# The attention loop of layers 1 to 3: scores copied by ScalarE, maximum on VectorE, subtraction on GpSimd

## The chip, the cores and the metric

The kernel runs on one core of a Trainium2 chip. The metric is the time of one execution on the device, in microseconds (us). Smaller is better. The engines are TensorE (matmul and transpose, results in PSUM), VectorE, ScalarE, GpSimd and SyncE, which only starts transfers here. Each engine works through its own list of instructions in order, and waits for the others on semaphores.

## The reference

Four layers, each a cross-attention from 2048 tokens (2 sequences of 1024, width 256) to 64 context rows per sequence, and then a feed-forward part (a plain and a routed one, experts, an FP4-quantised one, experts with a shared part). What the change touches is the attention of layers 1, 2 and 3. Here it is for layer 2; layer 1 is the same, layer 3 also has a mask.

```python
q = query @ Wq + bq
k = key @ Wk + bk
v = value @ Wv + bv
# 16 heads of 16 numbers
scores = jnp.einsum('bhqd,bhkd->bhqk', q, k) / jnp.sqrt(HEAD_DIM)
attn = jax.nn.softmax(scores, axis=-1)
out = jnp.einsum('bhqk,bhkd->bhqd', attn, v)
return out.transpose(0, 2, 1, 3).reshape(B, S, D_MODEL) @ Wo + bo
# and around it: x = x + tanh(g_xattn[l]) * attention(layernorm(x), context)
```

Layer 0 differs in one thing that matters: a bias from memory is added to its scores.

## The kernel before

The program is a row of phases with a barrier after most of them; `attention(l)` is built four times, once a layer. Everything stays in on-chip memory: X holds the tokens (16 tiles of 128 tokens), FA and RA are two large scratch areas. The weights, keys and queries are split into a high and a low part, and a product of two such operands is three matmuls (`split_matmuls`, L254).

After the queries of all tiles are there, each engine runs the same loop over slots. In slot s an engine does, in an order written by hand in its `work` function, its share for several tiles at once:

- TensorE (L802): transposes of the probabilities of tile s (L810); scores of a later tile, 12 small matmuls (L833), in layer 3 with four mask matmuls ahead of them (L826); transposes of the normalised output of tile s-1 (L842); product with V of tile s (L849); output projection of tile s-1 (L254), which waits for `ot_split`.
- ScalarE (L628): copy of the transposed probabilities of tile s out of PSUM (L631, into `pt`); high part of the transposed output of tile s-1 (L634, `ot`); exponential of tile s+1 (L639), which waits for `sub_done`.
- VectorE (L722): reciprocal of the row sums and normalisation of tile s-1 (L727, L728); output bias and residual of tile s-2 (L740, L742); maximum over each head's 64 scores and subtraction of it, for the tile that is LEAD ahead; low part of the transposed output of tile s-1 (L762), which waits for `ot_hi` and signals `ot_split`.

The tile of scores is 128 x 1024 numbers: 16 heads by 64 context rows. It lies in two of the eight PSUM banks, and there are two such pairs. In layers 1 to 3 LEAD is 1: VectorE reads the scores of tile s+1 in PSUM twice, for the maximum (L758) and for the subtraction (L759), whose result goes to one of two `probs` buffers. GpSimd has no part in these loops. In layer 0 LEAD is 2: VectorE adds the bias to the scores of tile s+2 while it moves them to one of three `probs` buffers (L750), takes the maximum there (L756), and GpSimd subtracts it (L572). TensorE computes scores LEAD+1 tiles ahead. Slots run from -LEAD-1 to 17.

The loop of layer 0 is written out slot by slot. In layers 1 to 3 `slots` writes out the first and the last slots and puts slots 2 to 11 of ScalarE and VectorE in a hardware loop of two slots a turn, whose counts of semaphores are computed in registers. TensorE's list is written out in all layers.

Of the kernel before, what the change touches and what calls it, by code (L numbers as in the profile page):

```python
# [76 lines left out]
def build(nc, A, out, stop=99):  # L77
    with ExitStack() as ctx:
# [368 lines left out]
        def attention(l):  # L447
# [10 lines left out]
            BUFS = 3 if first else 2  # L458
# [26 lines left out]
            bias_free, max_ready = shared(n_ + "biasfree"), shared(n_ + "max")  # L485
# [6 lines left out]
            LEAD = 2 if first else 1  # L492
            FIRST_SLOT, LAST_SLOT = -LEAD - 1, NT + 1
            LOOP = (1, NT // 2 - 2)
# [24 lines left out]
            def slots(eng, work, steps=None, per_slot=0):  # L519
                if first:  # L520
                    for t in range(FIRST_SLOT, LAST_SLOT + 1):
                        work(Slot(t - t % 2, t % 2), steps)
                    return steps.base + steps.n if steps else 0

                for t in range(FIRST_SLOT, 2 * LOOP[0]):
                    work(Slot(t - t % 2, t % 2), steps)
                before = steps.base + steps.n if steps else 0
                with eng.Fori(2 * LOOP[0], 2 * LOOP[1], 2) as t:
                    if steps:
                        steps = Steps(eng, dve_steps, per_slot * t + (before - 2 * per_slot * LOOP[0]))  # L530
                    for p in range(2):
                        work(Slot(t, p), steps)
                    assert not steps or steps.n == 2 * per_slot, (steps.n, per_slot)
                if steps:
                    steps = Steps(eng, dve_steps, before + 2 * per_slot * (LOOP[1] - LOOP[0]))
                for t in range(2 * LOOP[1], LAST_SLOT + 1):
                    work(Slot(t - t % 2, t % 2), steps)
                return steps.base + steps.n if steps else 0
# [25 lines left out]
            def gpsimd(pool):  # L564
                if first:
                    kv.gpsimd(pool)
                norm.gpsimd(pool)
                if first:
                    for t in range(NT):
                        pr = probs[t % BUFS].rearrange("p (h s) -> p h s", s=S2)  # L570
                        pool.wait_ge(max_ready, t + 1)
                        pool.tensor_tensor(pr, pr, mx[t % 2].unsqueeze(2).to_broadcast([P, H, S2]), ALU.subtract).then_inc(sub_done, 1)  # L572

            def scalar(act):
# [53 lines left out]
                def work(slot, steps):  # L628
                    if slot.has(0):
                        slot.wait(act, pt_ready, 0, 1)  # L630
                        act.activation(pt, PS[:, 4:6, :].rearrange("p b (c t) -> p (b c) t", t=P), ACT.Copy).then_inc(pt_sb, 1)  # L631
                    if slot.has(-1):
                        slot.wait(act, ot_ready, -1, 1)
                        act.activation(ot[:, 0], PS[:, 7, 0:D].rearrange("p (k t) -> p k t", k=KC), ACT.Copy).then_inc(ot_hi, 1)  # L634
                    if slot.has(1):
                        t, p = slot.tile(1)
                        slot.wait(act, sub_done, 1, 1)
                        pr = probs[t % BUFS] if first else probs[p]
                        act.activation(pr, pr, ACT.Exp).then_inc(p_ready, 1)  # L639
# [3 lines left out]
            def vector(dve):  # L643
# [78 lines left out]
                def work(slot, steps):  # L722
# [20 lines left out]
                    if slot.has(LEAD):  # L743
                        t, p = slot.tile(LEAD)
                        sc = PS[:, 2 * p:2 * p + 2, :].rearrange("p k (h s) -> p (k h) s", s=S2)
                        pr = (probs[t % BUFS] if first else probs[p]).rearrange("p (h s) -> p h s", s=S2)
                        slot.wait(dve, s_ready, LEAD, 1)
                        if first:
                            dve.wait_ge(bias_here[p], 16 * (t // 2 + 1))
# [4 lines left out]
                            if t >= 2:  # L754
                                dve.wait_ge(sub_done, t - 1)
                            dve.tensor_reduce(mx[p], pr, AX, ALU.max).then_inc(max_ready, 1)  # L756
                        else:
                            steps(dve.tensor_reduce(mx[p], sc, AX, ALU.max))  # L758
                            dve.tensor_tensor(pr, sc, mx[p].unsqueeze(2).to_broadcast([P, H, S2]), ALU.subtract).then_inc(sub_done, 1)  # L759
# [5 lines left out]
                per_slot = 3  # L765
                taken[0] = slots(dve, work, steps, per_slot)

            def tensor(pe):
# [33 lines left out]
                def work(slot, steps):  # L802
# [10 lines left out]
                    if slot.has(LEAD + 1):  # L813
# [3 lines left out]
                        if t >= 2:  # L817
                            if first:
                                pe.wait_ge(bias_free, 2 + t - 1)
                            else:  # L820
                                slot.wait(pe, sub_done, 2, -1)
# [1767 lines left out]
```

## Time and profile before

| | us |
|---|---|
| median of 3 runs | 1744.93 |
| lowest, highest run | 1736.59, 1745.95 |
| profiled execution, its own time | 1738.02 |
| profiled execution, its span | 1736.3 |

| engine, over the span | busy us | share |
|---|---|---|
| TensorE, matmuls | 1429.2 | 82% |
| TensorE, weight loads (overlap the matmuls) | 1329.2 | 77% |
| VectorE | 1301.9 | 75% |
| ScalarE | 734.3 | 42% |
| GpSimd | 364.7 | 21% |

The profile names the TensorE clock that was granted, as a share of 2.4 GHz; it has two levels, 1.00 and 0.50 (1.2 GHz), and was 0.887 on the average of the span. The shares above are averages over very different phases. The four attention loops take about 78 us of the span in layer 0, 87 and 86 in layers 1 and 2 and 97 in layer 3, and only layers 1 to 3 have code that the change touches. In the rows further down PE is TensorE's matmul, PEld its weight load, DVE VectorE, ACT ScalarE and POOL GpSimd. A bracket at the end of a row tells how long the engine had been idle before it and what ended that.

### The profile page before, as it was taken

What the parts mean: (1) busy time and instruction counts of PE and PEld (TensorE: products, weight loads), DVE (VectorE), ACT (ScalarE), POOL (GpSimd) and SP (SyncE); (2) the same over time, 40 slices, a digit from 0 to 9 for tenths busy, and PEclk for the clock granted to TensorE, in tenths of its full rate; (3) what the DMA queues carried; (4) which work ended last, traced back from release to release, by engine and by line L of the source; (5) the groups of instructions that cost most, each with busy time, mean ns of one, the idle gap of its engine ahead of it and who ended that gap; (6) DMA issues with size and microseconds to landing.
All of it is one profiled execution on the core that took longest, in us unless ns stands there. A gap on an engine that the chain in (4) does not pass through costs nothing.

```text
span 1736.3 us, 27180 instructions
## 1 busy us (share of the span) xinstructions
PE 1429.2 (82%) x10234; PEld 1329.2 (77%) x10234; DVE 1301.9 (75%) x2433; ACT 734.3 (42%) x1203; POOL 364.7 (21%) x290
## 2 busy tenths in 40 slices
PE   5894997897975799995894138977989999999995
PEld 4793886686965799995793137976878889999995
DVE  5777778778787487773888877987777848888882
ACT  4442341202433277773451312324433226766762
POOL 2231001001000167773000000001000013544532
PEclk8996998898995699998897558988996999999998
DMA  3231100000002477874001000000002027777783
GB/s 131 97 98 65 55 1 1 1 1 10 1 37 91 158 212 228 237 214 90 8 1 56 0 1 1 1 1 10 1 10 89 1 85 242 210 225 222 209 227 73
DMA packets 46675, 147.70 MB, mean 85 GB/s; under 512 B 11427, under 2 KB 24406, under 8 KB 36950
## 3 DMA queue, kind: packets, MB, share of 16 engines
q1 hardware_dynamic: 28918, 122.30, 20.1%
q0 software_dynamic: 17664, 24.13, 8.1%
q8 instruction: 62, 1.02, 0.2%
q14 instruction: 31, 0.25, 0.0%
HBM read 125.96 MB, written 22.54 MB: 86 GB/s over the span
## 4 chain that ended last, share of the span: by engine, by line
PE 71%; DVE 20%; ACT 3%; DMA 2%; issue 2%; POOL 1%; POOLq 1%; SPq 0%; DVEq 0%; ACTq 0%
PE PS L254 48%; PE PS L849 7%; PE PS L810 3%; PE PS L833 3%; PE PS L937 2%; DVE stats L182 2%; PE PS L230 2%; PE PS L1081 1%; PE PS L842 1%; DVE Y L2251 1%; DVE Y L2250 1%; PE PS L1442 1%; DVE FA L2252 1%; DVE Y L2243 1%; DVE FA L2237 1%
## 5 line engine op out<-in xcount | busy, mean ns | idle before, releaser
L254 PE MATMUL PS<-RA 128*128 128x256 f32 (+3 forms) x6456 | 967.5, 310 | 63.5 <-DVE RA L343 15.9
L254 PEld LDWEIGHTS PS<-RA 128*128 128x128 f32 x6456 | 887.8, 196 | 112.7 <-issue 27.2
L1353 POOL DMA_INDIRECT sum_rows<-Y,KT x92 | 164.1, 1784 | 185.7 <-ACT Y L1390 166.8
L1342 POOL DMA_INDIRECT Y<-normed_rows,KT x92 | 116.0, 1261 | 226.6 <-DVE KT L1156 157.8
L218 POOL TENSOR_TENSOR rstd<-vareps,neghalf 128x4 f32<-128x4 f32 x36 | 40.7, 1130 | 561.8 <-DVE vareps L187 453.9
L849 PE MATMUL PS<-VBF,FA 128*128 128x136 f32 x1024 | 135.6, 286 | 5.4 <-ACT FA L631 5.4
L849 PEld LDWEIGHTS PS<-VBF,FA 128*128 128x128 f32 x1024 | 124.1, 191 | 11.3 <-ACT FA L631 7.5
L1421 DVE TENSOR_TENSOR RA<-FA,RA 128x2048 fp32r<-128x2048 f32 x46 | 105.2, 2288 | 20.3 <-ACT RA L1382 20.3
L230 PE MATMUL PS<-ident,FA 128*128 128x128 f32 x160 | 33.5, 379 | 98.1 <-DVE FA L2252 40.7
L1369 ACT ACTIVATE FA<-PS,unit_bias 128x256 f32<-128x256 f32 x184 | 77.4, 476 | 86.7 <-PE PS L254 82.9
L631 ACT ACTIVATE FA<-PS 128x1024 f32<-128x1024 f32 x64 | 65.6, 1026 | 111.7 <-PE PS L810 111.7
L230 PEld LDWEIGHTS PS<-ident,FA 128*128 128x128 f32 x160 | 27.6, 198 | 103.7 <-issue 75.4
L1382 ACT ACTIVATE RA<-FA 128x2048 fp32r<-128x2048 f32 x46 | 88.1, 1915 | 18.8 <-DMA FA<-in_eup 18.8
L1487 DVE TENSOR_TENSOR RA<-FA,RA 128x1024 fp32r<-128x1024 f32 (+1 forms) x46 | 80.9, 1759 | 19.8 <-ACT RA L1414 19.8
L639 ACT ACTIVATE FA<-FA 128x1024 f32<-128x1024 f32 x64 | 67.5, 1055 | 40.5 <-DVE FA L759 35.1
L237 ACT ACTIVATE RA<-PS 128x512 fp32r<-128x512 f32 x64 | 36.7, 596 | 110.3 <-PE PS L230 110.2
L1805 DVE SCALAR_TENSOR_TENSOR X<-PS,coef,X 128x256 f32<-128x256 f32 x128 | 61.5, 483 | 25.8 <-PE PS L254 23.5
L810 PE MATMUL PS<-ident,FA 128*128 128x128 f32 x512 | 68.4, 278 | 12.0 <-ACT FA L639 12.0
L1414 ACT ACTIVATE RA<-FA 128x1024 fp32r<-128x1024 f32 (+1 forms) x46 | 68.5, 1489 | 0.0
L810 PEld LDWEIGHTS PS<-ident,FA 128*128 128x128 f32 x512 | 58.0, 143 | 12.8 <-ACT FA L639 12.8
L1462 DVE TENSOR_TENSOR RA<-FA,RA 128x512 fp32r<-128x512 f32 x92 | 63.7, 693 | 3.2
L833 PE MATMUL PS<-RA 64*128 64x256 f32 x768 | 63.6, 301 | 1.1 <-DVEq L753 1.1
(249 smaller groups left out, 1932.7 us busy)
## 6 DMA issues: line engine op xcount, KB each, us to landing
FA<-in_eup SPq DMA_DIRECT2D x46, 1024.0 KB, 7.4
FA<-in_edown SPq DMA_DIRECT2D x23, 1024.0 KB, 6.3
FA<-in_edown SPq DMA_DIRECT2D x23, 512.0 KB, 3.7
FA<-in_fside SPq DMA_DIRECT2D x16, 512.0 KB, 3.3
sum_rows<-X SPq DMA_DIRECT2D x2, 2048.0 KB, 7.4
normed_rows<-Y SPq DMA_DIRECT2D x2, 2048.0 KB, 7.2
X<-in_x SPq DMA_DIRECT2D x4, 512.0 KB, 9.2
FA<-in_up SPq DMA_DIRECT2D x4, 512.0 KB, 3.8
```

The costliest lines, as they stand in the source:

```text
L230: ins = pe.transpose(self.bank(g, k)[:, j * P:(j + 1) * P], self.normed(g, j)[:, 0, k * P:(k + 1) * P], ident[:, :])
L254: ins = pe.matmul(dst, stat(a, k), mov(b, k), start=(first and n == 0), stop=(last and n == len(todo) - 1))
L810: ins = pe.transpose(PS[:, 4 + c // 4, (c % 4) * P:(c % 4 + 1) * P], probs[t % BUFS][:, c * P:(c + 1) * P], ident[:, :])
L833: ins = pe.matmul(PS[:, 2 * p + r, k * COLS:(k + 1) * COLS], qs[rows, a, k, t * P:(t + 1) * P], kb[rows, b, m, k, r * COLS:(r + 1) * COLS] ...
L849: ins = pe.matmul(PS[:, 6, k * VC:(k + 1) * VC], pt[:, 4 * (c // 2) + 2 * k + c % 2, :], VB[:, t // HT, 4 * k + c, :], start=(c == 0), sto ...
L1342: pool.indirect_dma_start(out=rows_in[p][:, t, :], out_offset=None, in_=normed_rows, in_offset=bass.IndirectOffsetOnAxis(ap=source_of[:, R ...
L1353: pool.indirect_dma_start(out=sum_rows, in_=rows_out[p][:, t, :], in_offset=None, compute_op=ALU.add, out_offset=bass.IndirectOffsetOnAxis ...
L1369: ins = act.activation(h32[s % RING][:, c * BR:(c + 1) * BR], bank[:, c * BR:(c + 1) * BR], ACT.Relu, bias=unit_bias[:, p, 2 * s + c:2 * s ...
L1382: act.activation(up[q][:, 0], raw_up[q], ACT.Copy).then_inc(up_hi, 1)
L1414: act.activation(down[p][:, 0], raw_down[p], ACT.Copy).then_inc(down_hi, 1)
L1421: dve.tensor_tensor(up[q][:, 1], raw_up[q], up[q][:, 0].bitcast(F32), ALU.subtract).then_inc(up_ready, 1)
L1487: dve.tensor_tensor(down[p][:, 1], raw_down[p], down[p][:, 0].bitcast(F32), ALU.subtract).then_inc(down_ready, 1)
```

## The change

In layers 1 to 3:

- ScalarE copies the scores of tile s+2 from PSUM to a `probs` buffer, between the `ot` part of tile s-1 and the exponential of tile s+1. It signals the new semaphore `s_moved`.
- VectorE takes the maximum of tile s+2 from that buffer, after it has waited for `s_moved`. It no longer subtracts.
- GpSimd subtracts the maximum, in place.
- LEAD is 2, there are three `probs` buffers, and TensorE's scores of tile s+3 wait for `s_moved` of tile s+1 where they waited for `sub_done`.
- The hardware loop goes; all slots are written out.

Layer 0 keeps its code.

```diff
-            BUFS = 3 if first else 2
+            BUFS = 3
-            LEAD = 2 if first else 1
+            LEAD = 2
...
-            def slots(eng, work, steps=None, per_slot=0):
-                if first:
...
+            def slots(eng, work, steps=None):
+                for t in range(FIRST_SLOT, LAST_SLOT + 1):
                     work(Slot(t - t % 2, t % 2), steps)
                 return steps.base + steps.n if steps else 0
...
-                if first:
-                    for t in range(NT):
...
+                for t in range(NT):
+                    pr = probs[t % BUFS].rearrange("p (h s) -> p h s", s=S2)
+                    pool.wait_ge(max_ready, T + t + 1)
+                    pool.tensor_tensor(pr, pr, mx[t % 2].unsqueeze(2).to_broadcast([P, H, S2]), ALU.subtract).then_inc(sub_done, 1)
...
                         act.activation(ot[:, 0], PS[:, 7, 0:D].rearrange("p (k t) -> p k t", k=KC), ACT.Copy).then_inc(ot_hi, 1)
+                    if not first and slot.has(LEAD):
+                        t, p = slot.tile(LEAD)
+                        slot.wait(act, s_ready, LEAD, 1)
+                        act.activation(probs[t % BUFS].rearrange("p (r n) -> p r n", r=ROWTILES), PS[:, 2 * p:2 * p + 2, :], ACT.Copy
+                                       ).then_inc(s_moved, 1)
...
                     if slot.has(LEAD):
...
-                            steps(dve.tensor_reduce(mx[p], sc, AX, ALU.max))
-                            dve.tensor_tensor(pr, sc, mx[p].unsqueeze(2).to_broadcast([P, H, S2]), ALU.subtract).then_inc(sub_done, 1)
+                            dve.wait_ge(s_moved, NT * (l - 1) + t + 1)
+                        if t >= 2:
+                            dve.wait_ge(sub_done, T + t - 1)
+                        dve.tensor_reduce(mx[p], pr, AX, ALU.max).then_inc(max_ready, 1)
...
                             else:
-                                slot.wait(pe, sub_done, 2, -1)
+                                pe.wait_ge(s_moved, NT * (l - 1) + t - 1)
```

ScalarE's list in the last written-out slots of layer 1, before. A slot is three rows (`at_pt`, `at_ot` and `at_sub` are the semaphores `pt_ready`, `ot_ready` and `sub_done`):

```order
155 L631 ACTIVATE FA<-PS 128x1024 [waits at_pt]
156 L634 ACTIVATE RA<-PS 128x256 [waits at_ot]
157 L639 ACTIVATE FA<-FA 128x1024 [waits at_sub]
158 L631 ACTIVATE FA<-PS 128x1024 [waits at_pt]
159 L634 ACTIVATE RA<-PS 128x256 [waits at_ot]
160 L639 ACTIVATE FA<-FA 128x1024 [waits at_sub]
```

The same engine and layer in the change. A slot is four rows, lines L613, L616, L620 and L626 of the changed file:

```order
178 L613 ACTIVATE FA<-PS 128x1024 [waits at_pt]
179 L616 ACTIVATE RA<-PS 128x256 [waits at_ot]
180 L620 ACTIVATE FA<-PS 128x1024 [waits at_s]
181 L626 ACTIVATE FA<-FA 128x1024 [waits at_sub]
182 L613 ACTIVATE FA<-PS 128x1024 [waits at_pt]
183 L616 ACTIVATE RA<-PS 128x256 [waits at_ot]
184 L620 ACTIVATE FA<-PS 128x1024 [waits at_s]
185 L626 ACTIVATE FA<-FA 128x1024 [waits at_sub]
```

The copy of the scores (L620, waiting for `s_ready`) stands between the `ot` part and the exponential.

VectorE's list in one slot of layer 1, before: L727 and L728 normalise, L740 and L742 are bias and residual, L758 and L759 maximum and subtraction, L762 the low part of `ot`.

```order
541 L727 RECIPROCAL small<-PS 128x16 [waits at_o]
542 L728 TENSOR_TENSOR FA<-PS,small 128x256 [waits dve_steps]
543 L740 TENSOR_TENSOR FA<-PS,FA 128x256 [waits at_y]
544 L742 SCALAR_TENSOR_TENSOR X<-FA,gates,X 128x256 [waits dve_steps]
545 L758 TENSOR_REDUCE small<-PS 128x16 [waits at_s]
546 L759 TENSOR_TENSOR FA<-PS,small 128x1024 [waits dve_steps]
547 L762 TENSOR_TENSOR RA<-PS,RA 128x256 [waits at_othi]
```

And one slot of it in the change, where the lines are L714, L715, L727, L729, L744 (maximum) and L747 (`ot`):

```order
509 L714 RECIPROCAL small<-PS 128x16 [waits at_o]
510 L715 TENSOR_TENSOR FA<-PS,small 128x256 [waits dve_steps]
511 L727 TENSOR_TENSOR FA<-PS,FA 128x256 [waits at_y]
512 L729 SCALAR_TENSOR_TENSOR X<-FA,gates,X 128x256 [waits dve_steps]
513 L744 TENSOR_REDUCE small<-FA 128x16 [waits at_sub,at_smoved]
514 L747 TENSOR_TENSOR RA<-PS,RA 128x256 [waits at_othi]
```

The subtraction is gone, and the maximum, which waited for the scores of TensorE, now waits for `s_moved` of ScalarE and for `sub_done` of an earlier tile. The low part of `ot` still stands behind it.

## Rows read from the trace of the kernel before

**Rows 1.** Stretches (layer 1, layer 0, end of layer 1): us, busy per engine, granted clock, DMA

```profile
446.00:494.60 48.60, 48.60 (x442) 44.79 (x441) 42.93 (x71) 24.68 (x30) 0.00 (x0) 1.00 0.01 1
73.50:117.00 43.50, 43.50 (x399) 40.02 (x398) 34.25 (x55) 21.27 (x28) 17.48 (x10) 1.00 0.34 111
505.40:508.80 3.40, 2.69 (x22) 2.25 (x21) 1.90 (x5) 1.50 (x3) 0.00 (x0) 1.00 0.00 0
```

**Rows 2.** Chain of waits, 446 to 456 us (layer 1): its shares by line

```profile
by line: PE PS L849 42.7%; PE PS L833 18.2%; PE PS L810 17.5%; PE PS L254 15.1%; PE PS L842 7.4%
```

**Rows 3.** In order of time, layer 1: start us, us, engine, line, operation [idle before]

```profile
447.55 0.86 PEld L810 LDWEIGHTS PS<-ident,FA 128*128 128x128 f32 x8
...
448.68 1.02 ACT L631 ACTIVATE FA<-PS 128x1024 f32<-128x1024 f32 x1 [1.18 <-PE PS L810]
...
449.75 1.92 PEld L849 LDWEIGHTS PS<-VBF,FA 128*128 128x128 f32 x16
...
449.95 0.38 ACT L634 ACTIVATE RA<-PS 128x256 fp32r<-128x256 f32 x1 [0.25 <-PE PS L842]
...
450.04 1.22 DVE L759 TENSOR_TENSOR FA<-PS,small 128x1024 f32<-128x1024 f32 x1
...
451.18 0.41 DVE L762 TENSOR_TENSOR RA<-PS,RA 128x256 fp32r<-128x256 f32 x1
...
451.65 0.78 PEld L254 LDWEIGHTS PS<-RA 128*128 128x128 f32 x6
...
452.41 0.86 PEld L810 LDWEIGHTS PS<-ident,FA 128*128 128x128 f32 x8
```

**Rows 4.** In order of time, layer 0, the same columns

```profile
74.66 0.90 PEld L810 LDWEIGHTS PS<-ident,FA 128*128 128x128 f32 x8
...
76.67 1.22 DVE L756 TENSOR_REDUCE small<-FA 128x16 f32<-128x1024 f32 x1 [0.16 <-DVE FA L750]
...
77.11 0.38 ACT L634 ACTIVATE RA<-PS 128x256 fp32r<-128x256 f32 x1 [0.25 <-PE PS L842]
...
77.39 1.05 ACT L639 ACTIVATE FA<-FA 128x1024 f32<-128x1024 f32 x1
...
77.97 1.90 POOL L572 TENSOR_TENSOR FA<-FA,small 128x1024 f32<-128x1024 f32 x1 [2.63 <-DVE small L756]
...
79.08 0.26 DVE L727 RECIPROCAL small<-PS 128x16 f32<-128x16 f32 x1 [0.85 <-PE PS L849]
...
79.49 0.90 PEld L810 LDWEIGHTS PS<-ident,FA 128*128 128x128 f32 x8
```

**Rows 5.** Line L727 in layer 2, ns min/median/max, first and last start

```profile
L727 DVE RECIPROCAL small<-PS x11: 256/258/260, 864.6 to 913.2; 128x16 f32<-128x16 f32 x11
```

**Rows 6.** In order of time, layer 3, the same columns

```profile
1238.51 0.90 PEld L810 LDWEIGHTS PS<-ident,FA 128*128 128x128 f32 x8
...
1241.91 0.38 ACT L634 ACTIVATE RA<-PS 128x256 fp32r<-128x256 f32 x1 [1.19 <-PE PS L842]
...
1244.17 0.90 PEld L810 LDWEIGHTS PS<-ident,FA 128*128 128x128 f32 x8
```

**Rows 7.** In order of time, slot 14 of layer 1

```profile
500.87 0.90 PEld L810 LDWEIGHTS PS<-ident,FA 128*128 128x128 f32 x8
...
502.97 0.38 ACT L634 ACTIVATE RA<-PS 128x256 fp32r<-128x256 f32 x1
```

**Rows 8.** In order of time, starts of the loops of layers 1 and 3

```profile
427.45 0.69 ACT L586 ACTIVATE RA<-PS,small 128x512 fp32r<-128x512 f32 x1 [0.67 <-PE PS L254]
...
428.84 1.22 DVE L758 TENSOR_REDUCE small<-PS 128x16 f32<-128x1024 f32 x1
...
432.45 0.85 PEld L810 LDWEIGHTS PS<-ident,FA 128*128 128x128 f32 x8 [3.63 <-ACT FA L639]
...
435.02 2.85 PEld L849 LDWEIGHTS PS<-VBF,FA 128*128 128x128 f32 x16 [0.22 <-issue]
...
1201.88 1.22 DVE L758 TENSOR_REDUCE small<-PS 128x16 f32<-128x1024 f32 x1 [0.70 <-PE PS L833]
```

More of the change, by code:

```diff
@@ L484, in attention @@
             bias_here = [shared(n_ + f"bias{i}") for i in range(2)]
-            bias_free, max_ready = shared(n_ + "biasfree"), shared(n_ + "max")
+            bias_free, max_ready, s_moved = shared(n_ + "biasfree"), shared(n_ + "max"), shared(n_ + "smoved")
             norm = Norm(TURNS[f"at{l}"], X, xn, *[lambda g, k, a=a: xt[:, a, k, g % 2, :] for a in range(2)])
@@ L488, in attention @@
             Q = KC * NG * l
-            LEAD = 2 if first else 1
+            LEAD = 2
             FIRST_SLOT, LAST_SLOT = -LEAD - 1, NT + 1
-            LOOP = (1, NT // 2 - 2)
             class Slot:
@@ L517, in wait @@
                         eng.wait_ge(s, count)
-            def slots(eng, work, steps=None, per_slot=0):
-                if first:
[L521 to L536, printed above, removed]
+            def slots(eng, work, steps=None):
+                for t in range(FIRST_SLOT, LAST_SLOT + 1):
                     work(Slot(t - t % 2, t % 2), steps)
@@ L567, in gpsimd @@
                 norm.gpsimd(pool)
-                if first:
-                    for t in range(NT):
-                        pr = probs[t % BUFS].rearrange("p (h s) -> p h s", s=S2)
-                        pool.wait_ge(max_ready, t + 1)
-                        pool.tensor_tensor(pr, pr, mx[t % 2].unsqueeze(2).to_broadcast([P, H, S2]), ALU.subtract).then_inc(sub_done, 1)
+                for t in range(NT):
+                    pr = probs[t % BUFS].rearrange("p (h s) -> p h s", s=S2)
+                    pool.wait_ge(max_ready, T + t + 1)
+                    pool.tensor_tensor(pr, pr, mx[t % 2].unsqueeze(2).to_broadcast([P, H, S2]), ALU.subtract).then_inc(sub_done, 1)
             def scalar(act):
@@ L637, in work @@
                         slot.wait(act, sub_done, 1, 1)
-                        pr = probs[t % BUFS] if first else probs[p]
+                        pr = probs[t % BUFS]
                         act.activation(pr, pr, ACT.Exp).then_inc(p_ready, 1)
@@ L744, in work @@
                         t, p = slot.tile(LEAD)
-                        sc = PS[:, 2 * p:2 * p + 2, :].rearrange("p k (h s) -> p (k h) s", s=S2)
-                        pr = (probs[t % BUFS] if first else probs[p]).rearrange("p (h s) -> p h s", s=S2)
-                        slot.wait(dve, s_ready, LEAD, 1)
+                        pr = probs[t % BUFS].rearrange("p (h s) -> p h s", s=S2)
                         if first:
+                            slot.wait(dve, s_ready, LEAD, 1)
                             dve.wait_ge(bias_here[p], 16 * (t // 2 + 1))
@@ L753, in work @@
                             dve.sem_inc(bias_free, 1)
-                            if t >= 2:
-                                dve.wait_ge(sub_done, t - 1)
-                            dve.tensor_reduce(mx[p], pr, AX, ALU.max).then_inc(max_ready, 1)
-                        else:
-                            steps(dve.tensor_reduce(mx[p], sc, AX, ALU.max))
-                            dve.tensor_tensor(pr, sc, mx[p].unsqueeze(2).to_broadcast([P, H, S2]), ALU.subtract).then_inc(sub_done, 1)
+                        else:
+                            dve.wait_ge(s_moved, NT * (l - 1) + t + 1)
+                        if t >= 2:
+                            dve.wait_ge(sub_done, T + t - 1)
+                        dve.tensor_reduce(mx[p], pr, AX, ALU.max).then_inc(max_ready, 1)
                     if slot.has(-1):
@@ L763, in work @@
                                           ALU.subtract).then_inc(ot_split, 1)
-                per_slot = 3
-                taken[0] = slots(dve, work, steps, per_slot)
+                taken[0] = slots(dve, work, steps)
             def tensor(pe):
```

## The prediction

> **What bounds the kernel now.** I read the engine shares over the attention stretches first, then the chain of waits there, then the order of instructions in one slot (one pass of `work`, one tile of 128 tokens further along). In layer 1 TensorE's weight loads fill 44.79 of 48.60 us, its matmuls all of it, VectorE is busy 42.93, ScalarE 24.68, GpSimd not at all [rows 1]. VectorE looks almost as full as TensorE, so the reader should see which of the two is waited for: the chain of waits over two slots consists of TensorE lines alone [rows 2]. A slot takes 452.41 - 447.55 = 4.86 us, the distance between two groups of transposes (L810) [rows 3]. Layer 0 already works the way the change wants (scores copied to memory, maximum there, GpSimd subtracts), and its slot is 79.49 - 74.66 = 4.83 us [rows 4]. So both schemes stand at TensorE's pace, and the new one can win 0.03 us a slot at the most by relieving VectorE. Layer 2 is like layer 1: ten slots in 913.2 - 864.6 = 48.6 us, 4.86 each [rows 5]. Layer 3 (masked, four more matmuls a slot) takes 1244.17 - 1238.51 = 5.66 us [rows 6].
>
> TensorE's queue is in order: the transposes of slot s+1 stand behind the output projection (L254) of slot s, which waits for `ot_split`, VectorE's L762. Today L762 starts at 451.18 and L254 at 451.65, just when the product with V (L849, 16 loads of 1.92 us from about 449.75) is through [rows 3]. This cover is exactly used up: whatever makes L762 later moves TensorE one for one.
>
> **The change, part by part.**
>
> Removed from VectorE in each slot of layers 1 to 3: the subtraction L759, 1.22 us [rows 3]. The maximum stays at 1.22 us, now from memory as layer 0's L756 [rows 4]. VectorE was not the bound, so by itself this is worth nothing.
>
> Added to ScalarE: one copy of 128x1024 from PSUM. L631 is the same shape and direction, 1.02 us [rows 3]. ScalarE's load rises from 2.47 us a slot (24.68 over ten [rows 1]) to 3.5, inside 4.86. Added to GpSimd: the subtraction, 1.90 us as L572 [rows 4], also inside the slot.
>
> The place of the copy is what costs. In a slot s, ScalarE now runs: pt copy of tile s, `ot` high part of tile s-1 (L634), copy of scores s+2, exponential of s+1. VectorE runs: normalisation, residual, maximum of tile s+2, `ot` low part of tile s-1. Maximum and copy are of the same tile in the same slot, although the scores are two tiles ahead. So the maximum waits (on `s_moved`) until ScalarE has been through its pt copy, its `ot` part and its scores copy, and queued behind the waiting maximum stands the `ot` low part, for which TensorE's output projection waits, with the next transposes behind that. The buffers and the lead don't loosen this, since all of it lies within a slot. In layer 0 the copy's counterpart (the bias add) is VectorE's own and waits for no ScalarE work of the slot, which is why layer 0 doesn't show the loop.
>
> The new chain from one L810 to the next, for slots 1 to 12 of layers 1 and 2:
> - L810 to the start of L634: 77.11 - 74.66 = 2.45 us [rows 4] (2.40 in [rows 3]).
> - L634 to the next ScalarE operation, whose input is ready: 77.39 - 77.11 = 0.28 [rows 4].
> - the copy: 1.02.
> - copy to maximum: 0.16, the gap ahead of L756, which has a second wait as the new maximum has [rows 4]; the least hand-over in these rows is 0.05 (L631 ending 449.70, L849 starting 449.75 [rows 3]). I take the row of the like instruction.
> - maximum to the start of the `ot` low part: 451.18 - 450.04 = 1.14, as behind L759, which is as long [rows 3].
> - its start to L254: 451.65 - 451.18 = 0.47 [rows 3].
> - L254 to the next L810: 452.41 - 451.65 = 0.76 [rows 3].
> Sum 6.28 us, against 4.86: +1.42 a slot. The exponential of s+1 (starting at 2.45 + 0.28 + 1.02, 1.05 long [rows 4], so done by 4.8) and GpSimd's subtraction (5.2 to 7.1 us after the L810, needed two ScalarE operations into the next slot at 6.28 + 3.7) are off the path.
>
> Slot 13 still copies (tile 15) but has no scores to compute; L634 then follows the pt copy at 502.97 - 500.87 = 2.10 us as in slot 14 of layer 1 [rows 7], so it takes 2.10 + 3.83 = 5.93. Slot 0 has no `ot` part, slots 14 to 16 no copy: these keep their length. Per layer 1 or 2: 12 x 1.42 + (5.93 - 4.86) = 18.1 us.
> Layer 3: L634 starts 1241.91 - 1238.51 = 3.40 after L810 [rows 6], so a slot is 3.40 + 3.83 = 7.23 against 5.66; 12 x 1.57 + (5.93 - 5.66) = 19.1 us.
>
> The start of each loop: before, the first maximum starts at 428.84 and the first transposes at 432.45 [rows 8]. After, TensorE's first scores are read by the copy, then come maximum, GpSimd and exponential. Against the old way (maximum, subtraction, exponential) this adds the copy 1.02, the gap 0.16, and 1.90 + 0.08 for GpSimd (77.97 after the maximum's end at 77.89 [rows 4]) in place of 1.22 + 0.03: 1.91 us. In layers 1 and 2 ScalarE is free earlier than VectorE (428.14 against 428.84 [rows 8]), and the copy can start once the scores are there, between the two; I take 0.4 us of it, the bounds being 0 and 0.7. In layer 3 the maximum already waits for the scores (1201.88 [rows 8]), and nothing is gained. So +1.5 twice and +1.9 once: 4.9 us. The third tile of scores computed ahead of time fits into this wait.
>
> Writing the loop out takes away register work, worth at the most the 0.03 us a slot named above, and only if TensorE's pace ruled: zero here. More instructions are fetched; layer 0 is written out already and shows no cost of it.
>
> Sum: 18.1 + 18.1 + 19.1 + 4.9 = 60.2 us. With 0.05 in place of 0.16 at the gap and 2.40 in place of 2.45 it is 60.2 - 39 x 0.16 = 54; with what either can be too small by (another 0.05 at two of the hand-overs) 64. Against the profiled execution (1738.02 us, span 1736.3) this gives 1798; that execution lies 6.9 us under the median of the runs, 1744.93. I forecast a median, so 1744.93 + 60.2 = 1805.
>
> **Rivals.**
> 1. Not slower: TensorE's pace goes on ruling. The mechanism would be that the copy, the maximum and the `ot` low part end before the product with V does, that is the chain from L810 to L254 stays under 4.1 us. For it speaks that VectorE is at 88% and loses 1.22 us a slot. The Trainium skill, Perfetto Trace Analysis, section Optimizing Scalar/DVE Operations, holds that work may well be moved to ScalarE or even GpSimd where VectorE is saturated, which is this case's intent; the trace agrees on the load and not on the wait. Time: 39 x (4.48 - 4.86) = -15 if TensorE closed the gaps of its loads (44.79 over ten slots), +5 for the starts: 1735, faster; with layer 0's pace, -1 + 5: 1749, the same. Against it: 2.45 + 0.28 + 1.02 + 1.22 alone are 4.97.
> 2. GpSimd holds VectorE up while it subtracts. If VectorE's `ot` low part waited for the whole of the 1.90 us, each slot would be 8.2 us: 39 x 1.9 = +74 more, 1879. Against it: in layer 0 L727 starts at 79.08 in the middle of GpSimd's 77.97 to 79.87 and takes its usual 0.26 [rows 4]. The Trainium skill, same section, warns that the two share a read port, so that moving work between them might not help; by that rule this rival's time would come, by layer 0's row nothing.
> 3. TensorE's clock falls. The new slot leaves TensorE idle some 1.4 us before L254. In layer 1's first slot at the lower level (1.2 GHz) the loads of L849 took 2.85 us against 1.92 [rows 3, 8]: 1.48 times. TensorE's part of the new chain is about 3.2 us; if every slot ran so, +1.5 x 39 = 60 more, 1865; if one in four, +15, 1820. Against it: at the end of layer 1 TensorE was busy 2.69 of 3.40 us, 79%, and the granted clock stayed at 1.00 [rows 1]; the new slot gives about 4.8 of 6.3, 76%.
>
> **How the numbers follow.** Forecast 84% (1805, 54 to 64 us of loss on a base anywhere in the runs of before, 1736.6 to 1746: 1791 to 1810). Rival 1: 7%, of it 3 faster and 4 the same. Rival 2: 3%. Rival 3: 6%, most of it the case of one slot in four. The range takes in the forecast's spread and rival 3's smaller case: 1787 to 1822. A measurement of this kernel can tell about 0.5% (9 us) from no change. Faster 0.03, same 0.04, slower 0.93.
>
> **What the profile after would show.** VectorE's maximum in layers 1 to 3 should be waiting for the ScalarE copy, about 2 us in each slot; TensorE's L254 should be idle for `ot_split`, about 1.4 us in each of 13 slots a layer; L810 groups should be 6.3 us apart in layers 1 and 2 and 7.2 in layer 3; layer 0 should be as it was; the copy should take 1.03, the subtraction 1.90. The granted clock should stay at 1.00 in the loops. If L810 groups are 4.8 apart, the chain argument is wrong; if they are over 8, rival 2 holds; if matmuls are stretched, rival 3.

## The result, and the profile after

| | us |
|---|---|
| changed kernel, median of 4 runs | 1798.88 (1796.73 to 1800.08) |
| kernel before, median of 4 runs | 1741.66 (1736.59 to 1745.95) |
| ratio, with its 95% interval | 1.0336 (1.0310 to 1.0362) |
| profiled execution of the changed kernel, span | 1795.0 |

The change costs 57 us by the medians and 58.7 us by the two spans (1795.0 against 1736.3). The quotient of the two medians is 1.0329, inside the interval of the ratio. The same stretches as in [rows 1], of the changed kernel: layer 1 (463.5 to 500 us) and layer 3 (1260 to 1330 us). The columns are the stretch, its length, busy us of TensorE, its weight loads, VectorE, ScalarE and GpSimd, then the granted clock.

```profile
463.50:500.00 36.50, 30.44 (x266) 26.93 (x265) 18.30 (x36) 19.60 (x24) 11.33 (x7) 1.00 0.00 1
1260.00:1330.00 70.00, 58.82 (x479) 50.94 (x478) 30.15 (x60) 32.67 (x40) 18.74 (x10) 1.00 0.00 1
```

In layer 1 TensorE's matmuls now fill 30.44 of 36.50 us where they filled all of the time [rows 1]. No other engine took its place: VectorE is at 50%, ScalarE at 54%, GpSimd at 31%. When no engine is busy all of the time, what bounds the loop is a chain that passes through several of them. The chain of waits over three slots of layer 1, its shares by line:

```profile
by line: PE PS L254 20.7%; DVE small L744 19.3%; ACT FA L620 14.6%; PE PS L817 14.3%; PE PS L794 13.8%; ACT RA L616 6.1%; PE PS L826 6.0%; DVE RA L747 5.4%; issue 1.4%
```

Before, all of it was TensorE [rows 2]. Now VectorE's maximum (L744), ScalarE's copy of the scores (L620) and its `ot` part (L616) and VectorE's `ot` part (L747) make up 45%; the rest is TensorE's. One slot in order of time, the counterpart of [rows 3]: start, length, engine, line, operation, and in brackets how long the engine had been idle and for what.

```profile
469.62 0.90 PEld L794 LDWEIGHTS PS<-ident,FA 128*128 128x128 f32 x8
...
470.80 1.02 ACT L613 ACTIVATE FA<-PS 128x1024 f32<-128x1024 f32 x1 [2.59 <-PE PS L794]
...
472.06 0.39 ACT L616 ACTIVATE RA<-PS 128x256 fp32r<-128x256 f32 x1 [0.24 <-PE PS L826]
472.35 1.02 ACT L620 ACTIVATE FA<-PS 128x1024 f32<-128x1024 f32 x1
...
473.40 1.22 DVE L744 TENSOR_REDUCE small<-FA 128x16 f32<-128x1024 f32 x1 [2.53 <-ACT FA L620]
474.53 0.41 DVE L747 TENSOR_TENSOR RA<-PS,RA 128x256 fp32r<-128x256 f32 x1
474.70 1.91 POOL L554 TENSOR_TENSOR FA<-FA,small 128x1024 f32<-128x1024 f32 x1 [4.20 <-DVE small L744]
...
475.00 0.77 PEld L254 LDWEIGHTS PS<-RA 128*128 128x128 f32 x6 [1.21 <-DVE RA L747]
...
475.72 0.90 PEld L794 LDWEIGHTS PS<-ident,FA 128*128 128x128 f32 x8
...
476.48 0.49 DVE L729 SCALAR_TENSOR_TENSOR X<-FA,gates,X 128x256 f32<-128x256 f32 x1
```

The reader should follow the times downwards. The copy L620 ends at 473.37, the maximum L744 starts 0.03 us later after 2.53 us of waiting, L747 stands behind it although its own input (L616) had been there since 472.45, and TensorE's projection L254 has waited 1.21 us for L747. The next transposes come 475.72 - 469.62 = 6.10 us after the last ones. In layer 3 the same, in place of 5.66 us [rows 6]:

```profile
1280.20 0.90 PEld L794 LDWEIGHTS PS<-ident,FA 128*128 128x128 f32 x8
...
1283.58 0.38 ACT L616 ACTIVATE RA<-PS 128x256 fp32r<-128x256 f32 x1 [1.18 <-PE PS L826]
...
1286.51 0.78 PEld L254 LDWEIGHTS PS<-RA 128*128 128x128 f32 x6 [1.32 <-DVE RA L747]
...
1287.23 0.90 PEld L794 LDWEIGHTS PS<-ident,FA 128*128 128x128 f32 x8
```

A slot there is 1287.23 - 1280.20 = 7.03 us. The start of layer 1's loop, the counterpart of [rows 8]:

```profile
428.43 1.94 ACT L620 ACTIVATE FA<-PS 128x1024 f32<-128x1024 f32 x2 [0.22 <-PE PS L817]
429.50 0.78 PEld L817 LDWEIGHTS PS<-RA 64*128 64x128 f32 x12 [0.61 <-ACT FA L620]
...
430.85 3.76 POOL L554 TENSOR_TENSOR FA<-FA,small 128x1024 f32<-128x1024 f32 x2 [15.44 <-DVE small L744]
432.79 1.06 ACT L626 ACTIVATE FA<-FA 128x1024 f32<-128x1024 f32 x1 [2.42 <-POOL FA L554]
433.89 1.57 PEld L794 LDWEIGHTS PS<-ident,FA 128*128 128x128 f32 x8 [3.62 <-ACT FA L626]
```

From the first use of the scores (428.43) the chain goes over copy, maximum, GpSimd and exponential to the first transposes at 433.89.

Where the 58.7 us are, phase by phase (from the start of one phase's first statistics, L182, to the next one's, in both traces): attention of layer 1 17.2, of layer 2 18.9, of layer 3 19.8, the FP4 part between layers 2 and 3 2.9. Of the rest, the parts ahead of layer 1's attention differ by -0.9 to +0.4 and add up to 0.0, the others are within 0.2. The FP4 part has no changed instruction; its granted clock was 0.73 on the average, against 0.76 before. Why, the runs don't show: in the profiled executions of the other experiments this part is 0.0 to 4.4 us longer than before, by 1.1 with the written-out loops alone. So its 2.9 us, read from one execution of each kernel, can't be counted as a cost of the change.

### The profile page after: what moved, and what is told of

Read it like the earlier page. It is cut to its first block, busy times and chain, and to the rows that moved or that the text cites. A ratio compares the mean times of both kernels' runs of the same rounds, so it can differ in the third digit from the quotient of the medians.

```text
span 1795.0 us, 26949 instructions
## 1 busy us (share of the span) xinstructions
PE 1445.8 (81%) x10234; PEld 1335.9 (74%) x10234; DVE 1242.9 (69%) x2385; ACT 773.6 (43%) x1251; POOL 455.5 (25%) x338
## 4 chain that ended last, share of the span: by engine, by line
PE 65%; DVE 22%; ACT 6%; DMA 2%; issue 2%; POOL 1%; POOLq 1%; SPq 0%; DVEq 0%; ACTq 0%
PE PS L254 47%; PE PS L794 3%; PE PS L817 3%; PE PS L833 3%; DVE small L744 3%; ACT FA L620 2%; DVE stats L182 2%; PE PS L921 2%; PE PS L230 2%; PE PS L1065 1%; PE PS L826 1%; DVE Y L2235 1%; DVE Y L2234 1%; PE PS L1426 1%; ACT RA L616 1%
## 5 line engine op out<-in xcount | busy, mean ns | idle before, releaser
L254 PE MATMUL PS<-RA 128*128 128x256 f32 (+3 forms) x6456 | 972.0, 310 | 101.8 <-DVE RA L747 43.3
L254 PEld LDWEIGHTS PS<-RA 128*128 128x128 f32 x6456 | 891.0, 196 | 159.3 <-DVE RA L747 52.2
L554 POOL TENSOR_TENSOR FA<-FA,small 128x1024 f32<-128x1024 f32 x64 | 121.8, 1905 | 298.7 <-DVE small L744 298.6
L744 DVE TENSOR_REDUCE small<-FA 128x16 f32<-128x1024 f32 x64 | 77.9, 1220 | 132.0 <-ACT FA L620 129.3
L613 ACT ACTIVATE FA<-PS 128x1024 f32<-128x1024 f32 x64 | 65.6, 1025 | 157.2 <-PE PS L794 157.2
L794 PE MATMUL PS<-ident,FA 128*128 128x128 f32 x512 | 69.1, 280 | 11.7 <-ACT FA L626 11.7
L626 ACT ACTIVATE FA<-FA 128x1024 f32<-128x1024 f32 x64 | 67.6, 1057 | 8.8 <-POOL FA L554 8.8
L794 PEld LDWEIGHTS PS<-ident,FA 128*128 128x128 f32 x512 | 59.5, 144 | 12.5 <-ACT FA L626 12.5
```

What stands on the lines that cost most here:

```text
L254: ins = pe.matmul(dst, stat(a, k), mov(b, k), start=(first and n == 0), stop=(last and n == len(todo) - 1))
L794: ins = pe.transpose(PS[:, 4 + c // 4, (c % 4) * P:(c % 4 + 1) * P], probs[t % BUFS][:, c * P:(c + 1) * P], ident[:, :])
```

## The experiments

Theory A is that of the prediction: in each slot the `ot` low part stands in VectorE's queue behind a maximum that waits for ScalarE's copy. Theory B is that GpSimd's subtraction costs, by its length or by holding VectorE up. Theory C is TensorE's clock. In the table a slot is the distance of two groups of transposes in the middle of the loop.

| run | median us | ratio to before (95%) | slot, layers 1 and 2 | slot, layer 3 |
|---|---|---|---|---|
| before | 1741.66 | | 4.86 | 5.66 |
| changed | 1798.88 | 1.0336 (1.0310 to 1.0362) | 6.10 | 7.03 |
| copy_first | 1743.51 | 1.0019 (1.0003 to 1.0035) | 4.82 | 5.66 |
| copy_between | 1766.12 | 1.0147 (1.0117 to 1.0176) | 5.47 | 5.66 |
| low_part_first | 1759.62 | 1.0101 (1.0072 to 1.0130) | 5.41 | 5.65 |
| low_first_psum | 1746.19 | 1.0039 (1.0024 to 1.0054) | 4.83 | 5.65 |
| vector_subtracts | 1863.89 | 1.0688 (1.0646 to 1.0730) | 7.37, some 8.5 to 8.9 | 8.3 to 9.9 |
| pool_twice | 1803.55 | 1.0342 (1.0303 to 1.0380) | 6.10 | 7.03 |
| copy_twice | 1849.75 | 1.0607 (1.0559 to 1.0654) | 7.02, in each layer one of 8.21 | 7.9 to 9.5 |
| count_between | 1800.22 | 1.0322 (1.0282 to 1.0363) | 6.21 | 7.13 |
| before_written_out | 1738.83 | 0.9992 (0.9978 to 1.0006) | 4.81 | 5.66 |

Each ratio of an experiment is to runs of the kernel before on the same chip, whose median was 1738.6 to 1744.8, not the 1741.66 of the first row.

### The copy ahead of everything else in the slot

```diff
+                    if not first and slot.has(LEAD):
+                        t, p = slot.tile(LEAD)
+                        slot.wait(act, s_ready, LEAD, 1)
+                        act.activation(probs[t % BUFS].rearrange("p (r n) -> p r n", r=ROWTILES), PS[:, 2 * p:2 * p + 2, :], ACT.Copy
+                                       ).then_inc(s_moved, 1)
                     if slot.has(0):
                         slot.wait(act, pt_ready, 0, 1)
...
-                    if not first and slot.has(LEAD):
...
```

> The changed kernel, with one move in layers 1 to 3: ScalarE copies the scores of the tile two ahead as the first thing in the slot, ahead of the copy of the transposed probabilities. The scores are ready then, and the copy runs while TensorE transposes. Theory A: the maximum starts 0.9 us into the slot and is over before the high part is there, so TensorE's pace comes back: 4.83 and 5.66 us a slot, about 1746 us (1743 to 1751). Theory B: about 1799. If ScalarE's extra work were itself too much, the slot would be over 4.9 us here and in the kernel with the low part first.

Measured: 1743.51 us, slots of 4.82 and 5.66 us. Five rows of a slot of layer 1; L614 is the copy of the scores, L744 the maximum, L621 and L747 the `ot` parts:

```profile
466.35 1.02 ACT L614 ACTIVATE FA<-PS 128x1024 f32<-128x1024 f32 x1
...
467.50 0.90 PEld L794 LDWEIGHTS PS<-ident,FA 128*128 128x128 f32 x8
...
468.67 1.21 DVE L744 TENSOR_REDUCE small<-FA 128x16 f32<-128x1024 f32 x1
...
469.95 0.38 ACT L621 ACTIVATE RA<-PS 128x256 fp32r<-128x256 f32 x1 [0.25 <-PE PS L826]
...
470.37 0.43 DVE L747 TENSOR_TENSOR RA<-PS,RA 128x256 fp32r<-128x256 f32 x1 [0.49 <-ACT RA L621]
```

The copy starts before the slot's transposes, the maximum starts at 468.67, and the low part L747 now waits for nothing but the high part (469.95 plus 0.38, then 470.37). All operations of the changed kernel are there, with ScalarE's extra copy and GpSimd's subtraction. The place of the copy alone made 55 us. The kernel is still no faster than the one before: the interval of its ratio, 1.0003 to 1.0035, lies just above 1.

### The copy between the two other ScalarE copies

```diff
-                    if slot.has(-1):
-                        slot.wait(act, ot_ready, -1, 1)
...
                     if not first and slot.has(LEAD):
                         t, p = slot.tile(LEAD)
...
+                    if slot.has(-1):
+                        slot.wait(act, ot_ready, -1, 1)
...
```

> The changed kernel, with one move in layers 1 to 3: ScalarE copies the scores between the copy of the transposed probabilities and the high part of the transposed output, not behind both. Theory A, in numbers from the trace of the changed kernel: the copy starts 2.10 us after the transposes, not 2.73, so the maximum ends at 4.37, the low part starts at 4.28 and the projection at 4.75: a slot of 5.47 us in layers 1 and 2 (6.10 in the changed kernel, 4.86 before); in layer 3 the projection is no longer waited for and TensorE's own 5.66 us come back. Total about 1741.7 + 26 x 0.61 + 5 = 1762 us (1757 to 1767). Theory B: no change, about 1799.

```profile
471.14 0.90 PEld L794 LDWEIGHTS PS<-ident,FA 128*128 128x128 f32 x8
...
473.24 1.02 ACT L617 ACTIVATE FA<-PS 128x1024 f32<-128x1024 f32 x1
...
474.29 1.22 DVE L744 TENSOR_REDUCE small<-FA 128x16 f32<-128x1024 f32 x1 [1.90 <-ACT FA L617]
...
475.43 0.41 DVE L747 TENSOR_TENSOR RA<-PS,RA 128x256 fp32r<-128x256 f32 x1
...
475.89 0.77 PEld L254 LDWEIGHTS PS<-RA 128*128 128x128 f32 x6 [0.58 <-DVE RA L747]
...
476.61 0.46 PEld L794 LDWEIGHTS PS<-ident,FA 128*128 128x128 f32 x4
```

The copy (L617) starts 2.10 us after L794, the maximum 3.15, the low part 4.29, the projection 4.75, and the slot is 476.61 - 471.14 = 5.47 us, as worked out ahead (to 0.01 us). Layer 3 is back at TensorE's 5.66, since its projection comes later than 4.75 anyway. The time, 1766.12 us, is 4 above the expected one; the span of its profiled execution is 1759.1, and the runs went from 1760.78 to 1769.56. That the same edit moves two loops by different amounts, each by what its own pace leaves over, is the strongest evidence for theory A.

### The low part ahead of the maximum

```diff
+                    if not first and slot.has(-1):
+                        slot.wait(dve, ot_hi, -1, 1)
+                        dve.tensor_tensor(ot[:, 1], PS[:, 7, 0:D].rearrange("p (k t) -> p k t", k=KC), ot[:, 0].bitcast(F32),
+                                          ALU.subtract).then_inc(ot_split, 1)
                     if slot.has(LEAD):
...
-                    if slot.has(-1):
+                    if first and slot.has(-1):
```

> The changed kernel, with one move in layers 1 to 3: VectorE does the low part of the transposed output (the operation for which TensorE's output projection waits) ahead of the maximum that waits for ScalarE's copy, not behind it. All operations stay. Theory A (the low part is stuck in VectorE's queue behind the waiting maximum): TensorE's pace comes back, 4.83 us a slot in layers 1 and 2, 5.66 in layer 3; only the longer starts of the loops stay, about 5 us, so about 1746 us (1743 to 1751) where the kernel before takes 1741.7 and the changed one 1798.9. Theory B (GpSimd's subtraction, or the port it shares with VectorE, is what costs): nothing of it is moved, so 1790 or more. Theory C (TensorE's clock): the idle time would be gone too, so it can't be told from A here.

Measured: 1759.62 us, which is 14 us more than the 1746 of theory A and outside its range. Most of the loss is gone, but slots are 5.41 us, not 4.83. The chain of waits from 470 to 486 us has no projection in it any more:

```profile
by line: DVE X L729 24.1%; DVE small L748 22.9%; ACT FA L620 17.3%; ACT RA L616 9.6%; DVE FA L715 8.0%; PE PS L830 7.9%; DVE FA L727 6.4%; issue 4.3%; DVE small L714 3.3%
```

A slot of it; L748 is the maximum, L732 the low part:

```profile
477.36 0.87 PEld L798 LDWEIGHTS PS<-ident,FA 128*128 128x128 f32 x8
...
477.69 1.90 POOL L554 TENSOR_TENSOR FA<-FA,small 128x1024 f32<-128x1024 f32 x1 [3.50 <-DVE small L748]
...
478.15 0.41 DVE L727 TENSOR_TENSOR FA<-PS,FA 128x256 f32<-128x256 f32 x1
...
478.61 1.27 DVE L729 SCALAR_TENSOR_TENSOR X<-FA,gates,X 128x256 f32<-128x256 f32 x1
480.00 0.20 PEld L830 LDWEIGHTS PS<-ident,FA 128*128 128x128 f32 x2 [0.82 <-issue]
...
480.89 0.42 DVE L732 TENSOR_TENSOR RA<-PS,RA 128x256 fp32r<-128x256 f32 x1 [1.01 <-ACT RA L616]
...
482.77 0.87 PEld L798 LDWEIGHTS PS<-ident,FA 128*128 128x128 f32 x8
```

The residual update L729 takes 1.27 us. It took 0.48 before and in the changed kernel (476.48 above). It ends at 479.88, while GpSimd's subtraction (L554) ran from 477.69 to 479.59. The same holds in all 39 slots in which the two meet. L727, which also ran inside that time, took its usual 0.41. The transposes of the output, L830, wait for L729. So a second chain came up: maximum, normalisation, residual update, L830, high part, copy, maximum. In the changed kernel GpSimd starts at 474.70 and is through by 476.61. L729 starts 0.13 us before that, at 476.48, and still takes its 0.48 to 0.49 us, in all 39 slots, so this didn't show there. From this I formed theory D: a VectorE operation with both its operands in memory is held up while GpSimd works in memory. L729 is one; L727 has an operand in PSUM.

### The same with one operand of the residual update in PSUM

The kernel is that of the run before, with these lines changed on top:

```diff
-                            steps(dve.tensor_tensor(tmp, y, bo_row, ALU.add))
+                            steps(dve.tensor_tensor(y, y, bo_row, ALU.add))
...
-                            dve.scalar_tensor_tensor(x, tmp.unsqueeze(1), gates[:, l:l + 1], x, ALU.mult, ALU.add).then_inc(fin_done, 1)
+                            dve.scalar_tensor_tensor(x, y.unsqueeze(1), gates[:, l:l + 1], x, ALU.mult, ALU.add).then_inc(fin_done, 1)
```

> The run with the low part first gave slots of 5.41 us, not 4.83, and its trace shows the residual update (L729, which reads tmp and X, both in memory) taking 1.27 us in place of 0.48; it ends 0.3 us after GpSimd's subtraction does. Here that kernel is changed in one thing: the output bias is added in place in PSUM, so the residual update reads one operand from PSUM and one from memory. Theory D (an operation of VectorE with two operands in memory is held while GpSimd's subtraction runs, one with a single operand in memory is not): the update takes about 0.5 us, the chain through it is 5.41 - 0.8 = 4.6 us, under TensorE's pace, so slots of 4.83 us in layers 1 and 2 and 5.66 in layer 3, about 1744 us (1741 to 1750). Theory E (the update is late for another cause, its place in the slot or a wait): it stays at 1.27 us and the slot at 5.41, about 1760 us.

```profile
476.84 0.90 PEld L798 LDWEIGHTS PS<-ident,FA 128*128 128x128 f32 x8
...
477.10 1.90 POOL L554 TENSOR_TENSOR FA<-FA,small 128x1024 f32<-128x1024 f32 x1 [2.92 <-DVE small L748]
...
478.01 0.48 DVE L729 SCALAR_TENSOR_TENSOR X<-PS,gates,X 128x256 f32<-128x256 f32 x1
...
478.81 0.20 PEld L830 LDWEIGHTS PS<-ident,FA 128*128 128x128 f32 x2
```

L729 lies wholly inside GpSimd's subtraction (477.10 to 479.00) and takes 0.48 us, again in all 39 slots. The slot is 4.83 us, the time 1746.19. Theory D holds: the update was held because both its operands lay in memory while GpSimd worked there. The Trainium skill, SBUF — State Buffer, section "SBUF: two separate sides", says that a VectorE instruction with two SBUF inputs and a GpSimd instruction that reads SBUF exclude each other for the whole instruction, and that whichever starts first goes on. These two runs agree, 1.27 against 0.48 us.

### VectorE subtracts

```diff
-                for t in range(NT):
+                for t in range(NT if first else 0):
                     pool.wait_ge(max_ready, T + t + 1)
...
+                            steps(dve.tensor_reduce(mx[p], pr, AX, ALU.max))
+                            dve.tensor_tensor(pr, pr, mx[p].unsqueeze(2).to_broadcast([P, H, S2]), ALU.subtract).then_inc(sub_done, 1)
```

> The changed kernel, but in layers 1 to 3 VectorE subtracts the maximum itself, from memory, right behind the maximum; GpSimd does nothing in these loops. ScalarE still copies. Theory A: the subtraction, 1.22 us and a hand-over of 0.03, stands ahead of the low part too, so each of 39 slots gets 1.25 us longer: 7.35 us in layers 1 and 2, 8.29 in layer 3, +49 us; the starts lose about 2 us; about 1846 us. Theory B (GpSimd is what costs): faster than the changed kernel's 1799.

Measured: 1863.89 us. Theory B is out: without any work on GpSimd the loop got slower, and by the expected 1.25 us in most slots (7.37). The other 18 us weren't expected; the slots that are longer than 7.37 and 8.3 us add up to about 20 us in the profiled execution. Two pairs of rows from layer 1, and the stretches of layers 1 and 3:

```profile
460.57 0.78 PEld L254 LDWEIGHTS PS<-RA 128*128 128x128 f32 x6 [2.47 <-DVE RA L751]
...
461.29 1.36 PEld L798 LDWEIGHTS PS<-ident,FA 128*128 128x128 f32 x8
...
469.45 0.77 PEld L254 LDWEIGHTS PS<-RA 128*128 128x128 f32 x6 [2.58 <-DVE RA L751]
...
470.17 0.90 PEld L798 LDWEIGHTS PS<-ident,FA 128*128 128x128 f32 x8
```

```profile
446.00:526.00 80.00, 57.41 (x464) 50.88 (x466) 44.11 (x73) 33.22 (x41) 0.00 (x0) 0.94 0.00 1
1295.00:1390.00 95.00, 71.19 (x490) 61.44 (x489) 43.14 (x71) 33.67 (x42) 0.00 (x0) 0.87 0.00 1
```

The first L798 takes 1.36 us where it otherwise takes 0.90, and this slot is 470.17 - 461.29 = 8.88 us. The granted clock was 0.94 and 0.87 on the average of these stretches, so TensorE ran at 1.2 GHz for a part of them. TensorE was idle 2.47 us before L254 here, against 1.21 in the changed kernel, where the clock stayed at 1.00 in the middle of the loops. Rival 3 of the prediction is real, but in these runs it shows only where TensorE idles for longer than this change makes it.

### The copy twice

```diff
                         slot.wait(act, s_ready, LEAD, 1)
...
+                        act.activation(fview(4096, ROWTILES, COLS * KC), PS[:, 2 * p:2 * p + 2, :], ACT.Copy).then_inc(twice, 1)
                         act.activation(probs[t % BUFS].rearrange("p (r n) -> p r n", r=ROWTILES), PS[:, 2 * p:2 * p + 2, :], ACT.Copy
```

> The changed kernel, but in layers 1 to 3 ScalarE copies the scores twice, first into a spare buffer that nobody reads. Theory A: everything ahead of VectorE's maximum in a slot is on the path one for one. Two ScalarE operations in a row start 0.92 us apart or, with a wait of one for the other, about 1.05 us: 39 slots and 3 starts with 0.92 to 1.05 us more, +39 to +44 us, 1838 to 1843 us, slots of 7.0 to 7.15 us in layers 1 and 2. Theory B: no change.

Measured: 1849.75 us, slots of 7.02 in layers 1 and 2, which is 0.92 more than 6.10. One for one. In layer 3 the slots were 7.9 to 9.5 where 7.03 + 0.92 = 7.95 was due. The stretches of layers 1 and 3 show why:

```profile
445.00:505.00 60.00, 44.55 (x390) 39.50 (x387) 24.99 (x50) 36.22 (x44) 16.57 (x9) 1.00 0.00 1
1285.00:1380.00 95.00, 73.49 (x512) 63.06 (x510) 31.24 (x61) 45.15 (x55) 19.11 (x11) 0.87 0.00 1
```

Clock 1.00 in this stretch of layer 1, 0.87 in layer 3. Behind the stretch, from 515.0 to 523.2 us, it fell to 0.79 in layer 1 too: that is its one slot of 8.21 us. All the slots above 7.02 and 7.95 us add up to about 13 us, which makes up the 7 to 12 us above the expected range.

### GpSimd's subtraction twice

```diff
                     pool.wait_ge(max_ready, T + t + 1)
+                    if not first:
...
+                        pool.tensor_tensor(fview(4096, H, S2), pr, mx[t % 2].unsqueeze(2).to_broadcast([P, H, S2]), ALU.subtract
+                                           ).then_inc(twice, 1)
                     pool.tensor_tensor(pr, pr, mx[t % 2].unsqueeze(2).to_broadcast([P, H, S2]), ALU.subtract).then_inc(sub_done, 1)
```

> The changed kernel, but in layers 1 to 3 GpSimd does the subtraction twice, first into a spare buffer that nobody reads. Theory A: GpSimd is off the path. Its result is there 8.9 us after the transposes of the slot and wanted 9.75 us after them: no change in the slots (6.10 and 7.04 us), and 1.9 us more at the start of each loop, where the first exponential waits for it: about 1804 us. Theory B (GpSimd or the port it shares with VectorE): 39 slots with up to 1.9 us more, up to +74 us.

Measured: 1803.55 us, slots unchanged at 6.10 and 7.03. The increase lies in the starts: the attention phases of the profiled execution are 2.5, 1.4 and 3.0 us longer than in the changed kernel. (By the intervals the two times can't be told apart.) GpSimd has its slack in the loops, as worked out. The rows below are the residual update (L735) and the two subtractions (L558, L560):

```profile
472.78 0.48 DVE L735 SCALAR_TENSOR_TENSOR X<-FA,gates,X 128x256 f32<-128x256 f32 x1
472.86 2.17 POOL L560 TENSOR_TENSOR FA<-FA,small 128x1024 f32<-128x1024 f32 x1
...
477.10 1.90 POOL L558 TENSOR_TENSOR FA<-FA,small 128x1024 f32<-128x1024 f32 x1 [2.07 <-DVE small L750]
```

The second subtraction takes 2.17 us, 0.27 more than the first. It was due when L735 had just started, and it was GpSimd that was held this time. In the loops this is so in each of the 36 slots in which the two meet; where they don't, it takes 1.90 us.

### A count between wait and maximum

```diff
                             dve.wait_ge(s_moved, NT * (l - 1) + t + 1)
+                            dve.sem_inc(shared(n_ + "spare"), 1)
```

> The changed kernel, but in layers 1 to 3 VectorE increases a spare semaphore between the wait for the copy and the maximum, as layer 0 increases bias_free between its add and its maximum. The prediction took 0.16 us for the hand-over from copy to maximum, from layer 0; the changed kernel shows 0.03 with two waits. If the increase between is what costs 0.13 us, the gap ahead of the maximum is 0.16 us here and 39 slots are 0.13 us longer: +5 us, about 1804 us. If not, the gap stays 0.03 and the slot 6.10.

```profile
471.47 1.02 ACT L620 ACTIVATE FA<-PS 128x1024 f32<-128x1024 f32 x1
...
472.63 1.22 DVE L745 TENSOR_REDUCE small<-FA 128x16 f32<-128x1024 f32 x1 [2.64 <-ACT FA L620]
```

The copy ends at 472.49 and the maximum starts at 472.63: 0.14 us, where the changed kernel has 0.03. The slot is 6.21 us, 0.11 longer; in layers 1 and 2 one slot each took 6.56. So of layer 0's 0.16 us it is the increase of a semaphore between wait and operation that costs, not a second wait. The time, 1800.22 us, can't be told from the changed kernel's by the intervals; the slots can. The 5 us that the expectation named are thus not shown in the time.

### The loops of the kernel before, written out

```diff
             def slots(eng, work, steps=None, per_slot=0):
...
-                with eng.Fori(2 * LOOP[0], 2 * LOOP[1], 2) as t:
...
+                for t in range(FIRST_SLOT, LAST_SLOT + 1):
                     work(Slot(t - t % 2, t % 2), steps)
```

> The kernel before, with its loops of layers 1 to 3 written out slot by slot and nothing else changed. It measures what that part of the change is worth: a slot of 4.83 us in place of 4.86 in 10 slots of layers 1 and 2, nothing in layer 3 (TensorE's pace): -0.6 us, within what can be measured, 1741 us. If fetching the longer instruction lists cost something, it would be slower than the kernel before.

Measured: 1738.83 us, ratio 0.9992 with an interval that holds 1. The slots of layers 1 and 2 are 4.81 instead of 4.86 us. Writing out costs nothing, and what it gives (some 0.5 us in layer 1 and in layer 2, nothing in layer 3) is below what can be told in the time.

## Why the prediction was right, step by step

- **What bounds.** TensorE's pace, with the cover of L762 exactly used up. Shown: every run in which the low part was early enough came back to 4.82 or 4.83 us, none below, though VectorE had 1.2 us less to do.
- **The chain.** Right in every link. copy_first, copy_between and copy_twice move it by what the sum says (to TensorE's pace, to 5.47, by 0.92), pool_twice doesn't move it. The waits were forecast in kind and roughly in size: 2.53 us ahead of the maximum where it said about 2, 1.21 ahead of L254 where it said about 1.4. One count in the prediction is off without consequence: the exponential that needs GpSimd's result stands three ScalarE operations into the next slot, not two. The result was there 7.0 us after the transposes and wanted after 9.7.
- **Its size.** 6.28 us forecast, 6.10 measured; 7.23 and 7.03 in layer 3; 5.93 and 5.74 in slot 13. The term that was too large is the hand-over from copy to maximum, taken as 0.16 us from L756 [rows 4] on the ground that both have a second wait; it is 0.03, and count_between shows what the 0.13 in layer 0 are. The rest is L254 to the next transposes, 0.72 and not 0.76 (the sum took it from [rows 3]; layer 0 has 0.73), and 0.01 in three other links. The loops cost 15.9 + 15.9 + 16.6 = 48.4 us, not 18.1 + 18.1 + 19.1 = 55.3.
- **The starts.** 4.9 us forecast. From TensorE's first scores to the first transposes it is +1.38, +1.38 and +1.78 us, 4.5 in all. The chain from the first use of the scores grew by 1.85 us in each layer (1.91 forecast), and ScalarE's earlier start won back 0.48 in layers 1 and 2, where 0.4 was taken without a row that gives it. In layer 2 the first slot took 6.17 us against 5.27, at the lower clock for longer.
- **Not in the sum.** 2.9 us in the FP4 part, 0.8 in the first slots (+0.9 in that of layer 2), and 2.1 us around the loops, where no instruction changed and the lower clock covers other parts: 0.9 ahead of layer 3's loop (granted clock 0.73 against 0.79 before), 0.7 and 0.5 behind the last transposes of layers 2 and 3. They are differences of two single executions, and with the FP4 part some of this may be scatter. So the sum of 60.2 met the difference of spans of 58.7 with loops 7 us too dear and nearly 6 us that it didn't have. That the two nearly cancel is luck; the links of the chain are not.
- **The base.** 1805 was made on the median of three runs, 1744.93. With a fourth run it is 1741.66, and against the profiled execution the sum gave 1798, close to the measured 1798.88. The stated range held it either way.
- **Rival 1** (not slower): out. Its condition, a chain under 4.1 us, is what copy_first makes true, and there the time is 1743.51, close to the 1749 of its second case, which was reckoned from a base of 1744.93; the kernel before took 1738.8 on that chip.
- **Rival 2** (GpSimd holds VectorE): not in this kernel, but I had dismissed it by a row that can't speak on it. L727 of layer 0 [rows 4], the reciprocal, has a single operand and that in PSUM. An operation with two operands in memory is held, as low_part_first shows; in the changed kernel the only such operation in reach, the residual update, starts when GpSimd has 0.13 us left, and isn't held. The prediction doesn't ask where that update falls.
- **Rival 3** (the clock): not in the middle of the loops here, with 1.2 to 1.3 us of idle time in each slot, but in the two runs with 2.1 to 2.6 us of it.

## What to carry to other kernels

When work moves to another engine, look at its place in both queues before its length: what waits behind the new wait, and who waits for that. Computing scores tiles ahead doesn't help if the copy that passes them on stands, in its slot, behind operations that wait for that same slot's work; the remedy is a line's position (55 us here), not less work. Before costing an offload at all, find the pace that remains without it: TensorE at 4.83 us left this one nothing to win.

## What the runs showed of the hardware that was not expected

- A VectorE operation with both operands in memory took 1.27 us in place of 0.48 while GpSimd subtracted in memory, and 0.48 once one of them lay in PSUM, each in 39 of 39 slots. An overlap with the last 0.13 us of GpSimd's record didn't hold it (0.48 to 0.49 us in the changed kernel). The other way round, GpSimd's subtraction took 2.17 us in place of 1.90 when VectorE's operation had started first.
- A semaphore increase between a wait and the next VectorE operation put the operation off by 0.11 us; two waits on one operation showed 0.03 us of hand-over.
- In loops with 2.1 to 2.6 us of TensorE idle time a slot the granted clock fell in a part of the slots (0.87 to 1.00 on the average of a stretch), with 1.2 to 1.3 us (the changed kernel) it stayed at 1.00 in the middle of the loops. The idle time alone doesn't decide it: in copy_twice, layer 1 had 2.1 us in each slot and lost the clock in one of them, layer 3 had 2.2 and lost it in most. Why, the runs don't show.
